# A fused delta-rule attention and expert layer on one core: outputs from the solutions' query rows, moved by DMA, in a pipeline of five stages

## The reference, cut to what matters

```python
def step(S, inp):
    qt, kt, vt, bt, gt = inp
    S = S * jnp.exp(gt)[..., None, None]
    for i in range(nh):                       # nh = 3
        kS = jnp.einsum('bhd,bhde->bhe', ki, S)
        S = S + bi[..., None, None] * (ki[..., None] * (vi - kS)[:, :, None, :])
    o = jnp.einsum('bhd,bhde->bhe', qt, S)
    return (S, o)
...
gate = (x @ Wg).reshape(b, t, h, dv)
o = o * jax.lax.rsqrt(jnp.mean(o * o, -1, keepdims=True) + 1e-05) * rms_weight
o = o * jax.nn.silu(gate)
return o.reshape(b, t, h * dv) @ Wo
```

## Time and profile before

| what | value |
|---|---|
| median of 3 runs | 5166.61 us (5148.94 to 5180.19) |
| profiled execution, its own time | 5161.06 us |
| its span, first to last instruction | 5157.6 us |
| PE busy | 4342.7 us, 84% |
| ACT busy | 4065.0 us, 79% |
| DVE busy | 3738.3 us, 72% |
| POOL busy | 1849.6 us, 36% |
| granted clock of PE, mean | 0.953 |
| queue of SP (q1) | 437.06 MB, 29.1% of 16 engines |

### The profile page before, as it was taken

One profiled execution on the slowest core, in us unless ns is written; L12 is line 12 of the kernel. 1 busy time (PEld: TensorE's weight loads), 2 busy tenths in 40 slices (PEclk: granted clock), 3 DMA queues, 4 the chain that ended last, 5 costly groups with the idle time before them and its releaser, 6 DMA issues. The chain is left out here.

```text
span 5157.6 us, 153750 instructions
## 1 busy us (share of the span) xinstructions
PE 4342.7 (84%) x49412; PEld 3861.6 (75%) x49412; DVE 3738.3 (72%) x10065; ACT 4065.0 (79%) x9155; POOL 1849.6 (36%) x1871
## 2 busy tenths in 40 slices
PE   2888888888888988888888888888888867599992
PEld 1788888787777888777788787888778755488881
DVE  6888888787777888777788887888888712244445
ACT  3999999898888999888899998999999811155552
POOL 3444444444443444334444443444444302200004
PEclk6999999999999999999999999999999977699996
DMA  5222222222222332222222222222223123366663
GB/s 230 66 84 68 60 71 77 71 65 71 70 63 51 74 79 64 64 70 70 63 64 71 72 74 58 82 71 60 67 75 79 35 75 103 114 220 234 234 235 124
DMA packets 322342, 474.22 MB, mean 92 GB/s; under 512 B 85888, under 2 KB 267136, under 8 KB 302720
## 3 DMA queue, kind: packets, MB, share of 16 engines
q1 hardware_dynamic: 304784, 437.06, 29.1%
q0 software_dynamic: 6144, 16.79, 1.0%
q10 hardware_dynamic: 10608, 10.23, 0.6%
HBM read 352.02 MB, written 107.75 MB: 89 GB/s over the span
## 5 line engine op out<-in xcount | busy, mean ns | idle before, releaser
L1126 DVE SCALAR_TENSOR_TENSOR conv_acc<-bank,c_cur,conv_acc 128x256 f32<-128x256 f32 x2688 | 1236.5, 476 | 8.5 <-ACT conv_acc L939 3.2
L1190 DVE CAST_PREDICATED xs_lev<-mask,bank 128x256 f16<-128x256 uint16 x1536 | 660.8, 430 | 350.5 <-PE bank L758 322.5
L694 PE MATMUL bank<-x_cur,w_cur 128*128 128x259 f16 (+1 forms) x6144 | 862.0, 276 | 39.3 <-DMA g_cur<-g_parts 24.5
L995 ACT ACTIVATE inv<-bank 128x256 f16<-128x256 f32 x1536 | 605.0, 394 | 24.4 <-PE bank L770 23.0
L694 PEld LDWEIGHTS bank<-x_cur,w_cur 128*128 128x128 f16 (+1 forms) x6144 | 537.5, 98 | 106.3 <-DMA g_cur<-g_parts 25.4
L1314 POOL TENSOR_TENSOR squares<-kq_t 128x768 f32<-128x768 f32 x128 | 187.9, 1468 | 1171.2 <-ACT kq_t L954 1171.2
L758 PE MATMUL bank<-inv,n_high 128*128 128x64 f16 x6144 | 434.2, 193 | 186.7 <-ACT inv L995 170.4
L1005 ACT ACTIVATE invt<-bank 128x256 f16<-128x256 f32 x1280 | 511.4, 399 | 29.7 <-PE bank L782 16.1
L758 PEld LDWEIGHTS bank<-inv,n_high 128*128 128x128 f16 x6144 | 325.1, 98 | 245.5 <-ACT inv L995 209.4
L832 PE MATMUL bank<-w_sol,k_rows 128*128 128x128 f32 x2048 | 403.0, 289 | 125.2 <-ACT w_sol L1015 113.9
L1212 DVE SCALAR_TENSOR_TENSOR state<-state,t_cur,bank 128x128 f32<-128x128 f32 x1024 | 339.0, 341 | 214.0 <-PE bank L832 214.0
(11 more groups left out here) (246 smaller groups left out, 12038.7 us busy)
## 6 DMA issues: line engine op xcount, KB each, us to landing
w_cur<-w_parts_scratch SPq DMA_DIRECT2D x128, 1024.0 KB, 7.1
ew<-e_parts_scratch SPq DMA_DIRECT2D x117, 896.0 KB, 6.3
x_cur<-x_parts_scratch SPq DMA_DIRECT2D x128, 259.0 KB, 7.1
x_slots<-no_rows SPq DMA_DIRECT2D x128, 256.0 KB, 5.9
e_parts_scratch<-e_pair SPq DMA_DIRECT2D x96, 224.0 KB, 2.8
y_scratch<-y_buf SPq DMA_DIRECT2D x128, 128.0 KB, 1.7
y_in<-y_scratch SPq DMA_DIRECT2D x32, 512.0 KB
rows<-x_slots SPq DMA_DIRECT2D x39, 256.0 KB, 5.5
```

The source lines that it names most:

```text
L694: last = mm(bank[i % 2][:, 0:PW], w_cur[k.i % 2][:, wp, kt, c * P:(c + 1) * P].bitcast(BF16 if wp else F16), x_cur[k.i % 2][:, xp, kt, 0:P ...
L995: a(half(inv[k.i % R_LEV][g][:], l, 0), packed(halves(LEVT), l), ACT.Copy).then_inc(t_kept.sem, 1)
L1126: v.scalar_tensor_tensor(acc, bank[at % 2][:, i:i + TB], c_cur[k.i % 2][:, c, i:i + 1], acc, ALU.mult, ALU.add).then_inc(tap_step.sem if i ...
L1190: v.copy_predicated(half(xs_lev[g][l - 1][:], l, 0), half(mask4[:, l], l, 0).bitcast(U16), packed(halves(LEVX), l)).then_inc(x_kept.sem, 1)
```

## The change

- `keep_w` keeps the solutions of all eight chunks of a block (w_sol holds eight tiles). A chunk's output is the last 32 rows of its solution, the query rows. The second product of `solve` is gone, and `keep_out`.
- `move_outputs` on SP copies these rows by four DMAs a block, SBUF to SBUF, 64 pieces of 512 bytes each, to o_rows, where a partition is one token. It stands behind `load_next` of the block three later.
- `square_outputs` on ACT squares and sums 128 features in each of two halves; `norms_q` on PE and `sum_squares` on DVE add squared queries. Logarithm and root are now of 128 x 2. `scale_outputs` on POOL scales, `turn_outputs` on PE transposes, `gated_outputs` on DVE gates and reads PSUM.
- On ACT one set that holds both logarithm and exponential is loaded ahead of the group `var_ln`, `exp_decay`, `key_ln`, `key_root`, `var_root`.
- There are five stages, k0 to k4, and new orders on PE, ACT, DVE and POOL. k_rows, v_rows and inv_t have four buffers in place of two. Some fifteen waits that others imply are gone, on ACT and DVE above all.

The diff, cut to its core. The tables of counts follow the new orders and are left out, as are the orders of PE and POOL; of the lists of ACT and DVE the lines of the new ones stand. In the new order of PE `residual(0, k1)` comes after `project(4, k0)`; then `turn_values(0)`, `update(4)`, `decays`, `fix(0)`, `norms`, two `from_state`, `gram(0)`. Its body ends with `update(6)`, `solve(2)`, `turn_first(1)`, `fix(1, k1)`, `turn_keys(0)`, `from_state(7)`, `update(2)`.

```diff
-R_ROWS = 2
-R_INV = 2
+R_ROWS = 4
+R_INV = 4
 R_GATE = 4
 R_SQ = 1
 R_LEV = 1
+STAGES = 5
+STORED = 5
 UNROLL = 32
-STAGES = 4
-STORED = 4
...
-w_sol = ring("w_sol", 2, [P, P], F32)
-o_raw = ring("o_raw", 2, [P, TB], F32)
-o_sq = sb("o_sq", [P, TB], F32)
-o_sum = sb("o_sum", [P, TB], F32)
-ln_v = sb("ln_v", [P, TB], F32)
-rstd = sb("rstd", [P, TB], F32)
-o_norm = sb("o_norm", [P, TB], F32)
+w_sol = ring("w_sol", 2, [P, UN, P], F32)
+o_rows = ring("o_rows", 2, [P, 2, P], F32)
+o_sq = sb("o_sq", [P, 2, P], F32)
+o_sum = sb("o_sum", [P, 2], F32)
+v_sum = sb("v_sum", [P, 2], F32)
+ln_v = sb("ln_v", [P, 2], F32)
+rstd = sb("rstd", [P, 2], F32)
+o_norm = sb("o_norm", [P, 2, P], F32)
...
+def move_outputs(n, i):
+
+    if not isinstance(n, int) or 0 <= n < NIT:
+        at_least(sp, scaled, n - 1)
+        sp.sem_inc(sp_waited, 1)
+        for c in range(4):
+            done(sp, sol_kept, 4 + c, n)
+            sp.sem_inc(sp_waited, 1)
+            sp.dma_start(o_rows[i % 2][c * CH:(c + 1) * CH], w_sol[i % 2][96:128, c::4, :]).then_inc(moved[i % 2], 16)
...
         load_next(tb, head)
+        move_outputs(B * H * tb + head - 3, head - 3)
...
-    mm(outputs(k)[:, c * CH:(c + 1) * CH], rhs[k.i % 2][:], inv_t[k.i % R_INV][:, c, 96:128],
-       start=True, stop=True)
     mm(chain(k), inv_t[k.i % R_INV][:, c], rhs[k.i % 2][:], start=True, stop=True).then_inc(sol_made.sem, 1)

 @at_stage
...
 def update(c, k):
     done(pe, sol_kept, c, k.n)
-    if c == UN - 1:
-        pe.wait_ge(out_kept, k.n + 1)
-    mm(chain(k), k_rows[k.i % R_ROWS][:, c], w_sol[k.i % 2][:], start=True, stop=True).then_inc(upd_made.sem, 1)
-
-@at_stage
-def variance(k):
-    pe.wait_ge(osum_made, k.n + 1)
-    free(pe, tt_made, tt_kept, "variance", k.n)
-    mm(LEVTT[:, 0:TB], eps_dh[:], o_sum[:], start=True, stop=True).then_inc(tt_made.sem, 1)
-
...
+def norms_q(k):
+    pe.wait_ge(q_squared, k.n + 1)
+    free(pe, rows_made, rows_kept, "queries", k.n)
+    for i in range(2):
+        last = mm(ROWS[:, i:i + 1], q_sq[k.i % R_GATE][:, 4 * i:4 * i + 4].rearrange("p a b -> p (a b)"),
+                  cst[:, C_ONES, 0:1], start=True, stop=True)
+    last.then_inc(rows_made.sem, 1)
+
+@at_stage
+def turn_outputs(k):
+    pe.wait_ge(scaled, k.n + 1)
+    free(pe, rows_made, rows_kept, "outputs", k.n)
+    for i in range(2):
+        last = nc.tensor.transpose(ROWS[:, i * P:(i + 1) * P], o_norm[:, i], cst[:, C_ID])
+    last.then_inc(rows_made.sem, 1)
+
...
 @at_stage
 def keep_w(c, k):
     done(act, sol_made, c, k.n)
-    a(w_sol[k.i % 2][:], chain(k), ACT.Copy).then_inc(sol_kept.sem, 1)
-
-@at_stage
-def keep_out(k):
-
-    done(act, sol_made, 7, k.n)
-    at_least(act, normed, k.n - 1)
-    at_least(act, osq_made, k.n - 1)
-    a(o_raw[k.i % 2][:], outputs(k), ACT.Copy, scale=1.0 / OUT_SCALE).then_inc(out_kept, 1)
+    a(w_sol[k.i % 2][:, c], chain(k), ACT.Copy).then_inc(sol_kept.sem, 1)
+
+@at_stage
+def square_outputs(k):
+    act.wait_ge(moved[k.i % 2], 64 * (k.turn(2) + 1))
+    done(act, rows_kept, "queries", k.n - 1)
+    for i in range(2):
+        last = a(o_sq[:, i], o_rows[k.i % 2][:, i], ACT.Square, accum_out=o_sum[:, i:i + 1])
+    last.then_inc(o_squared, 1)

 @at_stage
 def var_ln(k):
-    done(act, tt_made, "variance", k.n)
-    a(ln_v[:], LEVTT[:, 0:TB], ACT.Ln, bias=eps_var[:, 0:1]).then_inc(tt_kept.sem, 1)
+    done(act, rows_kept, "queries", k.n)
+    a(ln_v[:], v_sum[:], ACT.Ln, bias=eps_var[:, 0:1], scale=EPS_RMS * DH).then_inc(var_ln_made, 1)

 @at_stage
 def var_root(k):
-    done(act, tt_kept, "variance", k.n)
-    at_least(act, normed, k.n)
+    act.wait_ge(var_ln_made, k.n + 1)
+    at_least(act, scaled, k.n)
     a(rstd[:], ln_v[:], ACT.Exp, scale=-0.5).then_inc(rstd_made, 1)
...
+def body(k0, k1, k2, k3, k4):
     keep_t(2, 0, k1)
     keep_tt(2, 0, k1)
+    silu(6, k1)
     first_tap(1, k0)
     keep_t(1, 1, k1)
+    keep_tt(1, 1, k1)
+    first_tap(2, k0)
+    keep_t(3, 0, k1)
     keep_tt(3, 0, k1)
+    keep_t(2, 1, k1)
     keep_w(3, k2)
+    keep_tt(2, 1, k1)
+    keep_w(7, k3)
+    silu(1, k0)
     keep_t(4, 0, k1)
     keep_tt(4, 0, k1)
     first_tap(3, k0)
+    keep_t(3, 1, k1)
+    keep_tt(3, 1, k1)
     keep_t(5, 0, k1)
     silu(2, k0)
     keep_tt(5, 0, k1)
     first_tap(0, k0)
+    keep_t(4, 1, k1)
+    keep_tt(4, 1, k1)
+    square_outputs(k3)
     keep_t(6, 0, k1)
     keep_tt(6, 0, k1)
     silu(3, k0)
+    keep_w(4, k2)
     first_tap(4, k0)
     keep_res(0, k1)
     silu(0, k0)
+    nc.scalar.preload_act_table_set("natural_log_exp_and_others")
+    var_ln(k3)
+    exp_decay(k0)
+    key_ln(k0)
+    key_root(k0)
+    keep_t(5, 1, k1)
+    keep_w(0, k1)
     var_root(k3)
+    keep_tt(5, 1, k1)
     keep_w(5, k2)
+    first_tap(5, k0)
+    keep_t(6, 1, k1)
+    high(0, k0)
     silu(4, k0)
+    keep_w(1, k1)
+    keep_first(0, k0)
+    keep_res(1, k1)
+    first_tap(6, k0)
+    high(1, k0)
+    keep_tt(6, 1, k1)
+    keep_t(1, 0, k0)
+    keep_w(6, k2)
+    gate_silu(k0)
+    keep_tt(1, 0, k0)
+    keep_w(2, k1)
+    silu(5, k0)
+    keep_first(1, k0)
...
-def normalize(k):
-    dve.wait_ge(rstd_made, k.n + 1)
-    at_least(dve, gated, k.n)
-    v.scalar_tensor_tensor(o_norm[:], o_raw[k.i % 2][:], neg_rms[:, 0:1], rstd[:], ALU.mult, ALU.mult)\
-        .then_inc(normed, 1)
-
-def body(k0, k1, k2, k3):
-    system(1, k1)
-    mask_x(6, 1, k2)
-    tap(5, 1, k1)
+def sum_squares(k):
+
+    done(dve, rows_made, "queries", k.n)
+    dve.wait_ge(o_squared, k.n + 1)
+    at_least(dve, var_ln_made, k.n)
+    v.scalar_tensor_tensor(v_sum[:], o_sum[:], 1.0 / (EPS_RMS * DH * DH), ROWS[:, 0:2], ALU.mult, ALU.add)\
+        .then_inc(rows_kept.sem, 1)
+
+@at_stage
+def gated_outputs(k):
+    done(dve, rows_made, "outputs", k.n)
+    dve.wait_ge(gate_done, k.n + 1)
...
+def body(k0, k1, k2, k3, k4):
+    tap(6, 2, k1)
     new_state(6, k3)
+    keep_fix(1, k2)
+    tap(6, 3, k1)
     right_side(7, k3)
...
     tap(0, 1, k0)
+    sum_squares(k3)
+    tap(0, 2, k0)
...
-def out_square(k):
-    pool.wait_ge(out_kept, k.n + 1)
-    at_least(pool, osum_made, k.n)
-    tt(o_sq[:], o_raw[k.i % 2][:], o_raw[k.i % 2][:], ALU.mult).then_inc(osq_made, 1)
-
-@at_stage
-def out_sum(k):
-    pool.wait_ge(osq_made, k.n + 1)
-    pool.wait_ge(q_squared, k.n + 1)
-    done(pool, tt_made, "variance", k.n - 1)
-    tt(o_sum[:].rearrange("p (a b) -> p a b", a=UN), o_sq[:].rearrange("p (a b) -> p a b", a=UN),
-       q_sq[k.i % R_GATE][:], ALU.add).then_inc(osum_made, 1)
-
-@at_stage
-def gated_out(k):
-    pool.wait_ge(normed, k.n + 1)
-    pool.wait_ge(gate_done, k.n + 1)
-    at_least(pool, stored[k.i % 2], 16 * k.turn(2))
-    tt(y_buf[k.i % 2][:], o_norm[:], gate[k.i % R_GATE][:], ALU.mult).then_inc(gated, 1)
+def scale_outputs(k):
+    pool.wait_ge(rstd_made, k.n + 1)
+    done(pool, rows_made, "outputs", k.n - 1)
+    tt(o_norm[:], o_rows[k.i % 2][:], rstd[:, :, None].broadcast_to([P, 2, P]), ALU.mult).then_inc(scaled, 1)

```

More of the change, by code:

```diff
@@ L16 @@
-import math
 from contextlib import ExitStack
@@ L475, in build @@
             rows_made = Count("rows_made", (
-                (("keys", 0), 1), (("keys", 1), 1), (("values", 0), 1), (("values", 1), 1), ("norms", 0), (("gram", 0), 0),
-                (("gram", 1), 0)))
+                ("outputs", 4), (("keys", 1), 1), ("queries", 3), (("values", 0), 1), ("norms", 0), (("gram", 0), 0),
+                (("gram", 1), 0), (("values", 1), 1), (("keys", 0), 0)))
             t_made = Count("t_made", (
-                ((1, 1), 1), ((4, 0), 1), ((2, 1), 1), ((5, 0), 1), ((3, 1), 1), ((6, 0), 1), ((4, 1), 1), ((5, 1), 1),
@@ L512, in build @@
+                ((0, 2), 0), ((4, 1), 0), ((4, 2), 0), ((5, 1), 0), ((5, 2), 0), ((6, 1), 0)))
             tapped = Count("tapped", (
-                (5, 1), (6, 1), (1, 0), (2, 0), (3, 0), (0, 0), (4, 0)))
+                (6, 1), (1, 0), (2, 0), (3, 0), (0, 0), (4, 0), (5, 0)))
             rows_kept = Count("rows_kept", (
-                (("gram", 1), 1), (("keys", 0), 1), (("keys", 1), 1), (("values", 0), 1), (("values", 1), 1), ("norms", 0),
-                (("gram", 0), 0)))
+                (("keys", 0), 1), ("outputs", 4), (("keys", 1), 1), ("queries", 3), (("values", 0), 1), ("norms", 0),
@@ L663, in _ @@
                             load_next(tb, head)
+                            move_outputs(B * H * tb + head - 3, head - 3)
                     for head in range(B * H):
-                        body(NTB - 1, head)
-                        pieces(NTB - 1, head)
+                        body((NTB - 1), head)
+                        pieces((NTB - 1), head)
                         if head + 1 < B * H:
-                            load_next(NTB - 1, head)
-                    for i in range(STORED):
+                            load_next((NTB - 1), head)
+                        move_outputs(B * H * (NTB - 1) + head - 3, head - 3)
+                    for i in range(max(STORED, 4)):
                         body(NTB, i, new=False)
```

(22 more changed lines are left out.)

322 lines of the change are left out of this document (129 added, 193 removed).

## The result

The changed kernel takes 5213.15 us (median of 10 runs, 5184.84 to 5239.58), the kernel before 5160.59 beside it. The ratio is 1.0107, 95% interval 1.0075 to 1.014: about 1% slower. One of the ten runs of the kernel before, 5668.47 us, was in a slower state and is left out of the ratio. The forecast was 5115 us; the range held the time, the sign was wrong. The profiled execution has a span of 5211.1 us, where the one before had 5157.6.

The account below looks back on a forecast made before the run. ACT was taken to bound the loop; after the change a ring of 12.8 + 17.6 = 30.4 us, plus 0.45 for stalls, gains 50 us, less 5 for a drain: 5161 - 45 = 5115 us, range 4710 to 5440.

Parts of the forecast that it names:

- The bound before: Loop of the kernel before: ACT bounds it, busy 28.4 of 30.53 us a block, with PE close behind.
- The work: Busy time a block after the change: ACT 28.4 to 23.4 us, PE 27.4 to 25.5, DVE 25.2 to 24.7.
- The ring: Cycle once a block: tap(6, 3), load, moves, squares, second half, next tap; 30.4 us, a floor for the period.
- first leg: From the end of tap(6, 3) on DVE to moved rows landed: 12.8 us, bounds 7.3 and 16.3.
- The way to the first move: On SP, from x_cur's issue to t_cur's, whose place the moves take: 5.38 us.
- The landing: From issue to arrival behind the load, taken from t_cur's median: 6.3 us.
- The second leg: From the squares on ACT to the end of the next tap(6, 3): 17.6 us, bounds 16.3 and 21.
- 0.45 for stalls: Scattered stalls a block: 0.76 us, of which 0.3 hidden beside the transfer; mean period 30.9 us.
- The path: Section on the wait of the squares for moved rows; it ends in the sum 5161 - 45 = 5115 us.
- PE cools down in the wait: Rival, chance 0.28: PE stands some 4 us a block, then runs at half clock; 2.2 us a block, 5400 us.
- a wait of 4.8: ACT reaches its squares 8 us after the tap, then waits 4.8 us a block for the moved rows.
- The moves are in time: Rival, chance 0.23: rows land within ACT's 8 us; period 27.4 us, gain 400 us, total 4765 us.

Follow-up runs that it names:

- behind w_cur: The changed kernel with SP's load issued as w_cur, the four moves, x_cur, c_cur, g_cur: 4431.76 us, ratio 0.8644 to the kernel before.
- kept-warm kernel: The changed kernel with forty unused 128 x 128 matmuls on PE ahead of residual(0): 5024.69 us, ratio 0.9755 to the kernel before.
- The one set alone: The kernel before with only the set holding logarithm and exponential loaded ahead of key_ln: 4830.39 us, ratio 0.9371.

## Why the prediction was wrong

**The bound before: right.** 98% of two removed loads is in the time.

**The work: right in size.** Two loads a block as counted. The squares were taken at 0.5 and cost (76.9 + 47.9) / 128 = 0.98 by busy time; in ACT's timeline the next operation starts 0.6 after the first of them. PE's 25.5 us are met: over the loop it is busy 25.52 a block with the moves behind w_cur.

**The ring: right, with two terms of the first leg wrong in opposite directions.** The forecast was 12.8 us from the end of the tap; the turn above has 13.6, the mean is 12.54 from x_cur's issue, which comes 0.3 behind the tap in the median. The way to the first move is as taken (5.61 for 5.38). The landing was taken at 6.3 from t_cur and is 3.7. The moves were added at 0.9 as a transfer, and their issues alone take 3.63. I had counted that four DMAs "come behind load_next" for what is queued behind them on SP, and not for the squares, which need the last of them. That the two cancel is luck. The order on the queue, told in the forecast by the Trainium skill ("DMA: Bandwidth & Descriptors", on queues, rings and completion order), is not shown to be what delays them: on another queue, with the load as it was, the rows land in 4.6 us, ahead of the load in 2.0. What the runs show is time on SP, two terms of it: g_cur's long issue, which was inside the 5.38, and the moves' own.

**The second leg: right while PE is warm.** Forecast 17.6; with PE kept warm the mean is 18.11 - 0.3 from the squares to the end of the tap, the median 17.1. The kept-warm kernel's mean period is 30.40, stalls included, where the forecast had 30.4 and 0.45 for stalls. That it comes out to the first decimal is in part luck, by the two terms above.

**The failed step: the sum at the end of "The path", where the likeliest case left the clock out.** The rival "PE cools down in the wait" was written as another case, at 0.28, and the forecast's sum has nothing for the clock. Yet the forecast itself computed a wait of 4.8 and a standstill of PE of some 4 us in every block, and its own rows had half the clock behind a standstill of 3.3. By its own numbers both hold together. Measured are 3.76 us of wait in 119 blocks, a clock of 0.89 over the loop, at half behind the standstill that was looked at, and 1.49 us a block; the price had been taken at 2.2, between 1.7 and 3.4. The kept-warm kernel is what the forecast described: 2.5% faster than before, where it said 0.9%. The changed kernel is that plus 188 us. Put right term by term (the forecast's last sum, 5161 - 45, is 5116): 5115 + 1.49 x 128 for the clock - 0.5 x 128 for the mean ring (30.40, not 30.9) = 5242. The part of the span behind the last ln_k was 1037 us in the profile after and 1060 in the one before, which takes 22 more: 5220. It varies from 1011 to 1060 over the profiles, so the last few tens of us have no cause in the loop.

**"The moves are in time": right in mechanism, too slow.** It gave 27.4 us a block, from ACT's share of 93%. With the rows in time the period is 25.85 to 26.29 us, PE busy 98 to 99% of it. Why PE is kept fuller than ACT was is not shown.

**Two faster kernels.** Ahead of the load and behind w_cur are 13.1% and 13.6% below the kernel before; they ran beside different runs of it and their intervals overlap, so which of the two is better is open. Their profiled spans differ by 65 us, of which the loop has 22 (periods of 26.02 and 25.85 us); the rest lies behind it. In the same way behind x_cur and ahead of the load have the same time, but periods of 26.29 and 26.02 us. The one set alone, in the kernel before, gives nearly half of that (6.3%), with four loads a block left.

## What to carry to other kernels

When a small DMA is put behind a large load on one queue, add up the issues, its own too, down to the last piece that the reader needs, and then the landing; where that is longer than the time until it is read, put it ahead of the load or between its transfers. When the sum of a forecast contains a standstill of TensorE in every block, the clock behind it belongs into the sum and not among the rivals. An engine that issues DMAs itself stands for all of their issues (2.9 us for four on ACT): give them to one that nothing waits for.

## What was not expected of the hardware

- The fourth DMA of the load, behind x_cur (259 KB), w_cur (1 MB) and c_cur, takes long to issue, whichever transfer it is: g_cur 2.8 us in the median and 3.9 at the most, and in its place the first of the moves 2.5 and 3.9. With the moves between x_cur and w_cur g_cur takes 0.56 in the median, and the others of that load as little.
- The same 32 KB move lands in a median of 2.0, 3.0, 3.8, 4.8 or 3.7 us on an otherwise equal kernel, by what was issued ahead of it (nothing of the load, x_cur, w_cur, all but g_cur, all four), and in 4.6 on another queue. More ahead of it doesn't always mean a later landing.
- Work that nothing reads made the kernel 188 us faster: 333 us of it, in a place where PE stood. Where PE was busy 99% of the loop, the same work cost 276 us.
